# A fused Mamba-2 block on one core: the decay products taken from bf16 parts, and the second decay and attention moved one block later

## The chip, the core and the metric

The kernel runs on one NeuronCore of a Trainium2 chip. The metric is the device time in microseconds, the median of several runs. Shorter is better. The engines are TensorE (PE in the profile, its weight loads PEld), VectorE (DVE), ScalarE (ACT), GpSimd (POOL) and SyncE (SP, which issues all the DMAs here).

## The reference, cut to what matters

The input is 8 sequences of 256 tokens with 512 channels. Each goes through a layernorm, an RMS norm, a Mamba-2 mixer, a gated MLP of width 1792, a second layernorm, a linear layer with a routed LoRA and a last layernorm. The change touches the mixer's decay only:

```python
a = (dt * A).reshape(B, c, Q, H).transpose(0, 1, 3, 2)      # Q = 128 tokens a chunk, H = 4 heads
cs = jnp.cumsum(a, axis=-1)
tri = jnp.tril(jnp.ones((Q, Q), bool))
Ldec = jnp.where(tri, jnp.exp(cs[..., :, None] - cs[..., None, :]), 0.0)
att = jnp.einsum('bchqn,bchkn->bchqk', Cc, Bc) * Ldec
Yd = jnp.einsum('bchqk,bchkp->bchqp', att, Xdt)
...
Yo = jnp.einsum('bchqn,bchpn,bchq->bchqp', Cc, prev, jnp.exp(cs))
```

The exponent cs[q] - cs[k] is the sum of a over the tokens after k up to q. The kernel gets it as a matrix product: a mask times `ra`, where `ra` is a spread over the triangle (`ra[k, h, q] = a[k, h]` for k <= q). There are three such products in a sequence: one for each of the two chunks of 128 tokens, with the mask `below`, and one with the mask `ones` for exp(cs) of the second chunk.

## The kernel before

A sequence of 256 tokens is a group g, and there are 8. The work is a software pipeline of steps t = 1 to 9 (`steps`). In step t the mixer (part a) works on group t, the MLP (part b) on group t-1, and the last layers (part c) on group t-2. Group 0's mixer, together with the scaling and splitting of the weights, runs ahead of the steps in the functions `first`, and `head(g)` is true for group 0 alone.

A step has 14 blocks f = 0 to 13, one for each block of 128 MLP channels. Every engine has its own hand-written order of work. In block f each of PE, ACT and DVE first does its share of the MLP for f and then what the tables `A_AT` (mixer), `C_AT` (last layers) and `NEXT_AT` (next group) name for f. On PE the MLP's share is `b_gu(f)` (gate and up, 24 products into a bank of `GU`) and then `b_down(f-1)` (6 products into `ACC`). For block f ACT computes the silu (`b_silu`, L721), DVE multiplies (`b_prod`, L1111), ACT writes the upper half (`b_hi`, L731) and DVE the lower half (`b_lo`, L1116) of `act`, for which `b_down(f)` waits. `b_gu(f)` waits for `b_prod(f-2)`. Engines meet through semaphores, and each engine works strictly in its own order, so whatever stands behind a waiting instruction waits too.

GpSimd has no blocks. Its order in a step is: `norm_c(c, 1)` (L523: two tiny instructions that give the inverse deviation for a norm of part c), `b_copy` (L521), `a_xd` (L493: four products y = D * x), `a_scan_in` (L477: two instructions that write `ra`), `a_tdt` (L485: two instructions that spread dt over the triangle into `hn`), `norm_c(c, 2)`, `a_xw` (L500), `a_ce` (L508), `a_norm`, `a_rms` and `norm_c(c, 3)`.

These are the places around the change:

- DVE, block 2: `a_dt` ends with `a_t` (L1045), for which `a_scan_in` waits. Block 3: `a_h0` (L987) and `c_stats2`. Block 4: `c_h3` (L1140, which waits for `norm_c(c, 2)`) and `c_lo3` (L1162). Block 5: `a_dec` for both chunks (L1055, L1059) and `a_att` of the first (L1064). Block 6: `a_att` of the second and `c_route`.
- ACT, block 4: `a_tok`, both `a_exp` (L689) and then `c_hi3` (L737, after `c_h3`). Block 6: the third `a_exp`. Changes between Exp and Silu cost an ACT_TABLE_LOAD.
- PE, block 4: `a_tok`, `a_dec(0)`, `a_dec(1)`. Block 5: `a_att(0)`, `a_dec(2)`. Block 6: `a_att(1)`, `a_state` and `c_logits`. All matrix products show as L1368, the line of the helper `mm`.

A float32 product appears in the trace as two MATMUL records.

Of the kernel before, what the change touches and what calls it, by code (L numbers as in the profile page):

```python
# [102 lines left out]
def build(nc, x, w_in, w_dt, w_out, w_gate, w_up, w_down, w_lin, w_gl, lora_b, cols, rows, ln_rows, out):  # L103
# [3 lines left out]
    with ctx:  # L107
        def sb(name, shape, dt=F32):
            return ctx.enter_context(nc.sbuf_tensor(name, shape, dt))
# [6 lines left out]
        def sem(name):  # L116
            if name not in made:
# [41 lines left out]
        a_t = sb("a_t", [P, TILES, H])  # L159
        ra = sb("ra", [P, TILES, H, P])  # L160
        dec = sb("dec", [P, TILES, H, P])
# [14 lines left out]
        rows_1, rows_2, rows_3 = [t.bitcast(F16).rearrange("p (t s d) -> p t s d", t=TILES, s=2)  # L176
                                  for t in (ra[:].rearrange("p t h q -> p (t h q)"),
                                            xbc[:, 0:4].rearrange("p c q -> p (c q)"),
# [92 lines left out]
        def head(g):  # L271

            return g == 0
# [166 lines left out]
        def _(pool):  # L440
# [31 lines left out]
            def a_scan_in(g):  # L472
                pool.wait_ge(sem("a_ready"), g + 1)
                for j in range(TILES):
                    if j == 0:
                        prev(g, 3, 3, pool, sem("dec_ps_ready"))
                    nc.gpsimd.tensor_tensor(ra[:, j], tri[:].unsqueeze(1).broadcast_to([P, H, P]),  # L477
                                            a_t[:, j].unsqueeze(2).broadcast_to([P, H, P]), ALU.mult)\
                        .then_inc(sem("ra_ready"), 1)

            def a_tdt(g):
# [53 lines left out]
            def step(a, b, c):  # L535
                if c is not None and alone(c):
                    return
                if c is not None:
                    chain_c.group(c)
                    norm_c(c, 1, 1.0)  # L540
                if b is not None:
                    b_copy(b)
                if a is not None:
                    a_xd(a)
                    a_scan_in(a)
                    a_tdt(a)
                if c is not None:
                    norm_c(c, 2, ACT_SCALE)
                if a is not None:
                    a_xw(a)  # L550
                    a_ce(a)
                    if a + 1 < GROUPS:
                        a_norm(a + 1)
                    a_rms(a)
                if c is not None and not held(c):
                    norm_c(c, 3, 1.0)
                    chain_c.close()
# [28 lines left out]
        def _(eng):  # L586
# [165 lines left out]
            def c_u(g, j):  # L752
# [5 lines left out]
                    3: lambda g: (a_silu(g, 2), a_z(g, 1)),  # L758
                    4: lambda g: (a_tok(g), a_exp(g, 0), a_exp(g, 1)), 6: lambda g: (a_exp(g, 2), a_state(g)),
                    8: lambda g: a_sumsq(g, 0), 9: lambda g: a_sumsq(g, 1), 11: lambda g: a_hi2(g)}  # L760
# [72 lines left out]
        def _(dve):  # L833
            setup = Chain(dve, sem("dve_setup"), 0)
            setup.group(0)

            chain_a = Chain(dve, sem("dve_a"), 17)
            chain_stats = Chain(dve, sem("dve_stats"), 3)
            chain_c = Chain(dve, sem("dve_c"), 19)
# [190 lines left out]
            def a_dt(g):  # L1030
# [4 lines left out]
                for c in (0.0, 1.0 / 3, -0.5, 1.0):  # L1035
                    if c:
                        chain_a(nc.vector.scalar_tensor_tensor(t, t, c, e, ALU.add, ALU.mult))
                    else:
# [7 lines left out]
                                        ALU.mult).then_inc(sem("a_ready"), 1)  # L1046

            def flat(t):
                return t.rearrange("p h q -> p (h q)")
# [187 lines left out]
            def c_out(g):  # L1237
                c_norm(g, 3, h3, h3, sem("n3_ready"))
                for j in range(TILES):
# [3 lines left out]
            A_AT = {0: lambda g: a_conv(g, 0), 1: lambda g: (a_conv(g, 1), a_dtv(g)),  # L1243
                    2: lambda g: (a_conv(g, 2), a_dt(g)), 3: lambda g: a_h0(g),
                    5: lambda g: (a_dec(g, 0), a_dec(g, 1), a_att(g, 0)), 6: lambda g: a_att(g, 1),
                    7: lambda g: (a_y(g, 0), a_y(g, 1)), 8: lambda g: a_h1(g, 0),
# [5 lines left out]
            def step(a, b, c):  # L1252
# [4 lines left out]
                if a is not None:  # L1257
                    chain_a.group(a)
                for f in range(FBLK):
                    if a == 1:  # L1260
                        prepare(f)
                    if b is not None:
                        b_prod(b, f)
                        b_lo(b, f)
                    if a is not None and f in A_AT:
                        A_AT[f](a)
                    if c is not None and f in C_AT:
                        C_AT[f](c)
                    if a is not None and a + 1 < GROUPS and f in NEXT_AT:
                        NEXT_AT[f](a + 1)  # L1270
# [95 lines left out]
        def _(pe):  # L1366
# [95 lines left out]
            def a_dec(g, n):  # L1462
# [7 lines left out]
                else:  # L1470
                    pe.wait_ge(sem("exp_ready"), g * 3 + 1)
                mm(dec_bank(g, n)[:], (below if n < TILES else ones)[:], flat(ra[:, min(n, 1)]), True, True)\
                    .then_inc(sem("dec_ps_ready"), 1)

# [130 lines left out]
            def last():  # L1605
# [11 lines left out]
                for j in range(TILES):  # L1617
                    c_lora(LAST, j)

            A_AT = {0: lambda g: g > 1 and a_in(g, 1), 1: lambda g: (a_in(g, 2), a_dt(g)), 2: lambda g: a_z(g, 0),  # L1620
                    3: lambda g: a_z(g, 1), 4: lambda g: (a_tok(g), a_dec(g, 0), a_dec(g, 1)),
                    5: lambda g: (a_att(g, 0), a_dec(g, 2)), 6: lambda g: (a_att(g, 1), a_state(g)),
                    7: lambda g: (a_y(g, 0), a_y(g, 1)), 8: lambda g: a_o(g, 0), 9: lambda g: a_o(g, 1)}
# [124 lines left out]
```

## Time and profile before

| | us |
|---|---|
| median of 3 runs (795.97 to 797.41) | 795.98 |
| the profiled execution | 792.34 |
| its span, first to last instruction | 790.6 |

| engine | busy us | share of the span |
|---|---|---|
| PE | 755.6 | 96% |
| PEld | 532.0 | 67% |
| DVE | 485.1 | 61% |
| ACT | 332.5 | 42% |
| POOL | 152.7 | 19% |

Busy time is the union of the records of an engine. A timeline merges neighbouring instructions of one kind and gives the start, the time that the merged stretch took, engine, line, operation, output <- input, shapes and count. A bracket at its end tells how long the engine sat idle before it and what released it. Starts and durations are in us from the start of the span. The time of the profiled execution is 1.7 us above its span.

### The profile page before, as it was taken

What the parts mean: (1) busy time and instruction counts of PE and PEld (TensorE: products, weight loads), DVE (VectorE), ACT (ScalarE), POOL (GpSimd) and SP (SyncE); (2) the same over time, 40 slices, a digit from 0 to 9 for tenths busy, and PEclk for the clock granted to TensorE, in tenths of its full rate; (3) what the DMA queues carried; (4) which work ended last, traced back from release to release, by engine and by line L of the source; (5) the groups of instructions that cost most, each with busy time, mean ns of one, the idle gap of its engine ahead of it and who ended that gap; (6) DMA issues with size and microseconds to landing.
All of it is one profiled execution on the core that took longest, in us unless ns stands there. A gap on an engine that the chain in (4) does not pass through costs nothing.

```text
span 790.6 us, 13864 instructions
## 1 busy us (share of the span) xinstructions
PE 755.6 (96%) x5558; PEld 532.0 (67%) x5558; DVE 485.1 (61%) x1109; ACT 332.5 (42%) x607; POOL 152.7 (19%) x199
## 2 busy tenths in 40 slices
PE   3898989999999999999999999999999999999995
PEld 3676756677667866687656876578666876667752
DVE  5988877866545764476645765457644766255356
ACT  2944675536332562335523363325613264222221
POOL 1220411033110340015110330105210231001021
PEclk9999999999999999999999999999999999999996
DMA  8960000301003020210104020220202101031001
GB/s 313 388 223 1 1 27 1 80 2 40 15 14 94 1 55 1 54 55 27 28 1 82 28 54 1 31 77 1 56 0 54 55 2 27 1 80 31 25 0 54
DMA packets 60081, 41.12 MB, mean 52 GB/s; under 512 B 45680, under 2 KB 45808, under 8 KB 60016
## 3 DMA queue, kind: packets, MB, share of 16 engines
q1 hardware_dynamic: 60016, 40.22, 18.3%
q8 instruction: 44, 0.72, 0.4%
q14 instruction: 21, 0.17, 0.1%
HBM read 25.01 MB, written 4.19 MB: 37 GB/s over the span
## 4 chain that ended last, share of the span: by engine, by line
PE 84%; DVE 10%; ACT 2%; issue 1%; DMA 1%; POOL 0%; SPq 0%; ACTq 0%; DVEq 0%
PE gu L1368 34%; PE wa L1368 24%; PE acc L1368 19%; PE wc L1368 6%; DVE weights L938 3%; DVE xbc L1011 2%; DMA weights<-in_w_in 1%; DVE sg L1111 1%; DVE stats_a L1167 0%; ACT act L731 0%; ACT weights L604 0%; PE wc L1583 0%; DVE hn L1173 0%; DVE act L1116 0%; PE wa L1456 0%
## 5 line engine op out<-in xcount | busy, mean ns | idle before, releaser
L1368 PE MATMUL gu<-h2t,weights 128*128 128x256 f16 x2688 | 311.6, 273 | 1.0 <-DVE h2t L1105 1.0
L1368 PEld LDWEIGHTS gu<-h2t,weights 128*128 128x128 f16 x2688 | 260.2, 98 | 55.6 <-issue 19.3
L1368 PE MATMUL acc<-weights,act 128*128 128x512 f16 x672 | 163.4, 379 | 8.8 <-DVE act L1116 8.8
L1111 DVE SCALAR_TENSOR_TENSOR sg<-gu,bound,sg 128x256 f32<-128x256 f32 x112 | 53.6, 478 | 117.6 <-ACT sg L721 116.9
L721 ACT ACTIVATE sg<-gu,scale_inv 128x256 f32<-128x256 f32 x112 | 53.0, 473 | 159.8 <-PE gu L1368 159.6
L1368 PEld LDWEIGHTS acc<-weights,act 128*128 128x128 f16 x672 | 65.2, 98 | 66.2 <-DVE act L1116 10.9
L1368 PE MATMUL wa<-ht,weights 128*128 128x256 f16 x912 | 105.4, 273 | 0.4 <-DVE h L1079 0.4
L1368 PEld LDWEIGHTS wa<-ht,weights 128*128 128x128 f16 x912 | 89.0, 98 | 16.8 <-issue 0.8
L731 ACT ACTIVATE act<-sg 128x256 f16<-128x256 f32 x112 | 46.6, 416 | 90.8 <-DVE sg L1111 90.8
L1116 DVE TENSOR_TENSOR act<-sg,act 128x256 f16<-128x256 f32 x112 | 50.6, 451 | 54.1 <-ACT act L731 54.1
L1011 DVE SCALAR_TENSOR_TENSOR xbc<-wa,conv_ws,xbc 128x253 f32<-128x253 f32 (+1 forms) x132 | 57.3, 475 | 2.0 <-ACT xbc L643 0.5
L1368 PE MATMUL wa<-w_out_t,y 128*128 128x512 f32 x128 | 57.6, 592 | 0.0
L463 POOL TENSOR_SCALAR small_c<-mv_c 128x2 f32<-128x2 f32 x21 | 4.0, 192 | 223.8 <-DVE mv_c L955 223.8
L938 DVE SCALAR_TENSOR_TENSOR weights<-weights,scale_v 128x512 f16<-128x512 f32 x56 | 41.1, 787 | 6.0 <-ACT weights L604 5.8
L1368 PEld LDWEIGHTS wa<-w_out_t,y 128*128 128x128 f32 x128 | 24.2, 190 | 25.0 <-issue 23.0
L493 POOL TENSOR_SCALAR y<-xbc,rows_t 128x256 f32<-128x256 f32 x28 | 32.8, 1186 | 35.1 <-ACT xbc L654 35.1
L643 ACT ACTIVATE xbc<-wa,cols_t,conv_ws 128x256 f32<-128x256 f32 x48 | 24.3, 559 | 34.7 <-PE wa L1368 34.7
L604 ACT ACTIVATE weights<-weights,scale_v 128x512 f16<-128x512 f32 x56 | 36.3, 712 | 1.6 <-DVE weights L938 0.9
L699 ACT ACTIVATE hn<-h 128x512 f32<-128x512 f32 x16 | 10.1, 630 | 59.9 <-DVE h L1079 59.9
L463 POOL TENSOR_SCALAR small_a<-mv_a 128x2 f32<-128x2 f32 (+1 forms) x22 | 5.3, 239 | 149.2 <-DVE mv_a L955 94.8
L1368 PE MATMUL wc<-weights,h3t 128*128 128x512 f16 x144 | 33.0, 379 | 0.0
L1079 DVE TENSOR_TENSOR h<-wa,h 128x512 f32<-128x512 f32 x16 | 11.1, 691 | 35.4 <-PE wa L1368 35.3
(214 smaller groups left out, 822.8 us busy)
## 6 DMA issues: line engine op xcount, KB each, us to landing
xa<-in_x SPq DMA_DIRECT2D x9, 512.0 KB, 3.8
weights<-in_x SPq DMA_DIRECT2D x7, 512.0 KB, 3.7
out_x<-h SPq DMA_DIRECT2D x14, 256.0 KB, 2.4
weights<-in_w_in SPq DMA_DIRECT2D x5, 512.0 KB, 7.9
weights<-in_w_down SPq DMA_DIRECT2D x3, 768.0 KB, 12.8
weights<-in_w_gate SPq DMA_DIRECT2D x2, 1024.0 KB, 12.4
weights<-in_w_up SPq DMA_DIRECT2D x2, 1024.0 KB, 13.9
weights<-in_w_gate SPq DMA_DIRECT2D x2, 768.0 KB, 13.9
```

The source lines that it names most:

```text
L493: nc.gpsimd.tensor_scalar(y[:, h], xbc[:, 0], rowt[:, 4 + h:5 + h], None, ALU.mult)\
L604: nc.scalar.activation(Wh[:, u, 0], W[:, u + SHIFT], ACT.Copy, scale=sv[:, t:t + 1])\
L643: nc.scalar.activation(xbc[:, c], src[:, m * SEQ:(m + 1) * SEQ], ACT.Identity, bias=conv_b[:, c:c + 1], scale=cw[:, c * TAPS + TAPS - 1:c ...
L699: nc.scalar.activation(hn[:, j], h01[:, j], ACT.Square, accum_out=ss[:, 0, j:j + 1])\
L721: nc.scalar.activation(sg[:, f % 2], GU[f % 2][:, 0:SEQ], ACT.Silu, scale=inv_gate)\
L731: nc.scalar.activation(act[:, slot(f), 0], sg[:, f % 2], ACT.Copy)\
L938: nc.vector.scalar_tensor_tensor(Wh[:, u, 1], W[:, u + SHIFT], sv[:, t:t + 1], Wh[:, u, 0], ALU.mult, ALU.subtract).then_inc(split, 1)
L1011: ins = nc.vector.scalar_tensor_tensor(xbc[:, c, late:], conv_in(g, c)[:, 0:SEQ - late], cw[:, c * TAPS + k:c * TAPS + k + 1], xbc[:, c, l ...
L1079: nc.vector.tensor_tensor(h01[:, j], o_bank(g, j)[:], h01[:, j], ALU.add)\
L1111: nc.vector.scalar_tensor_tensor(sg[:, f % 2], GU[f % 2][:, SEQ:2 * SEQ], up_to_act, sg[:, f % 2], ALU.mult, ALU.mult).then_inc(sem("prod_ ...
L1116: nc.vector.tensor_tensor(act[:, slot(f), 1], sg[:, f % 2], act[:, slot(f), 0], ALU.subtract)\
L1368: return nc.tensor.matmul(dst, left, right, start=start, stop=stop)
```

## The change

For groups 1 to 7 `a` is split into three bf16 parts (four small DVE instructions, `a_parts_of`), GpSimd spreads all three over the triangle (`a_spread`, in place of `a_scan_in`), and each decay product becomes three bf16 products with bf16 masks, accumulated in one bank. In GpSimd's order `a_xd` goes behind the spread and `a_tdt`. `a_dec(1)` goes from block 4 to block 5 on PE, its `a_exp` from block 4 to 5 on ACT, and DVE's `a_dec(1)` from block 5 to 6. Group 0 is computed as before.

```diff
-        ra = sb("ra", [P, TILES, H, P])
+        a_parts = sb("a_parts", [P, TILES, 3, H], BF16)
+        a_rest = sb("a_rest", [P, TILES, H])
+        scan = sb("scan_in", [P, TILES, 3, H, P], BF16)
+        ra = scan[:].rearrange("p t n h q -> p (t n h q)")[:, 0:2 * TILES * H * P].bitcast(F32)\
+            .rearrange("p (t h q) -> p t h q", t=TILES, h=H)
...
             def a_scan_in(g):
                 pool.wait_ge(sem("a_ready"), g + 1)
                 for j in range(TILES):
-                    if j == 0:
-                        prev(g, 3, 3, pool, sem("dec_ps_ready"))
                     nc.gpsimd.tensor_tensor(ra[:, j], tri[:].unsqueeze(1).broadcast_to([P, H, P]),
...
+            def a_spread(g):
+                pool.wait_ge(sem("parts_ready"), g)
+                for j in range(TILES):
+                    if j == 0:
+                        pool.wait_ge(sem("dec_ps_ready"), g * 3)
+                    nc.gpsimd.tensor_tensor(
+                        scan[:, j].rearrange("p n h q -> p (n h) q"),
+                        upper(tri[:]).unsqueeze(1).broadcast_to([P, 3 * H, P]),
+                        a_parts[:, j].rearrange("p n h -> p (n h)").unsqueeze(2).broadcast_to([P, 3 * H, P]),
+                        ALU.mult).then_inc(sem("ra_ready"), 1)
...
                 if a is not None:
+                    a_spread(a)
+                    a_tdt(a)
                     a_xd(a)
-                    a_scan_in(a)
-                    a_tdt(a)
                 if c is not None:
                     norm_c(c, 2, ACT_SCALE)
...
-                    4: lambda g: (a_tok(g), a_exp(g, 0), a_exp(g, 1)), 6: lambda g: (a_exp(g, 2), a_state(g)),
+                    4: lambda g: (a_tok(g), a_exp(g, 0)), 5: lambda g: a_exp(g, 1), 6: lambda g: (a_exp(g, 2), a_state(g)),
...
+            def a_parts_of(g):
+
+                dve.wait_ge(sem("a_ready"), g + 1)
+                chain_p(nc.vector.tensor_copy(a_parts[:, :, 0], a_t[:]))
+                chain_p(nc.vector.tensor_tensor(a_rest[:], a_t[:], a_parts[:, :, 0], ALU.subtract))
+                chain_p(nc.vector.tensor_copy(a_parts[:, :, 1], a_rest[:]))
+                nc.vector.tensor_tensor(a_parts[:, :, 2], a_rest[:], a_parts[:, :, 1], ALU.subtract)\
+                    .then_inc(sem("parts_ready"), 1)
...
-                    2: lambda g: (a_conv(g, 2), a_dt(g)), 3: lambda g: a_h0(g),
-                    5: lambda g: (a_dec(g, 0), a_dec(g, 1), a_att(g, 0)), 6: lambda g: a_att(g, 1),
+                    2: lambda g: (a_conv(g, 2), a_dt(g), a_parts_of(g)),
+                    3: lambda g: a_h0(g),
+                    5: lambda g: (a_dec(g, 0), a_att(g, 0)), 6: lambda g: (a_dec(g, 1), a_att(g, 1)),
...
-                mm(dec_bank(g, n)[:], (below if n < TILES else ones)[:], flat(ra[:, min(n, 1)]), True, True)\
-                    .then_inc(sem("dec_ps_ready"), 1)
+                left, j = below if n < TILES else ones, min(n, 1)
+                if head(g):
+                    last = mm(dec_bank(g, n)[:], left[:], flat(ra[:, j]), True, True)
+                else:
+                    for part in range(3):
+                        last = mm(dec_bank(g, n)[:], upper(left[:]), flat(scan[:, j, part]), part == 0, part == 2)
+                last.then_inc(sem("dec_ps_ready"), 1)
...
-                    3: lambda g: a_z(g, 1), 4: lambda g: (a_tok(g), a_dec(g, 0), a_dec(g, 1)),
-                    5: lambda g: (a_att(g, 0), a_dec(g, 2)), 6: lambda g: (a_att(g, 1), a_state(g)),
+                    3: lambda g: a_z(g, 1), 4: lambda g: (a_tok(g), a_dec(g, 0)),
+                    5: lambda g: (a_dec(g, 1), a_att(g, 0), a_dec(g, 2)), 6: lambda g: (a_att(g, 1), a_state(g)),
```

## Rows read from the trace of the kernel before

**Rows 1.** The page: busy time of each engine and its share of the span.

```profile
PE 755.6 (96%) x5558; PEld 532.0 (67%) x5558; DVE 485.1 (61%) x1109; ACT 332.5 (42%) x607; POOL 152.7 (19%) x199
```

**Rows 2.** Windows: stretch, length, busy of PE, PEld, DVE, ACT, POOL, granted clock, DMA.

```profile
87.00:168.00 81.00, 74.42 (x510) 52.39 (x509) 60.47 (x116) 47.83 (x85) 14.61 (x14) 1.00 0.11 27
260.00:351.00 91.00, 91.00 (x664) 64.17 (x662) 53.23 (x123) 37.24 (x68) 18.88 (x23) 1.00 0.15 36
```

**Rows 3.** Timeline of PE, blocks 4 to 6 of step 3 (group 3).

```profile
279.44 1.46 PE L1368 MATMUL acc<-weights,act 128*128 128x512 f16 x6
...
281.06 1.88 PE L1368 MATMUL wa<-ra,below 128*128 128x512 f32 x4
282.78 2.78 PE L1368 MATMUL gu<-h2t,weights 128*128 128x256 f16 x24
285.40 1.46 PE L1368 MATMUL acc<-weights,act 128*128 128x512 f16 x6
286.69 1.02 PE L1368 MATMUL wa<-xbc 128*128 128x512 f32 x2
...
291.03 1.46 PE L1368 MATMUL acc<-weights,act 128*128 128x512 f16 x6
```

**Rows 4.** Timeline of DVE in the same stretch, blocks 2 to 5.

```profile
276.15 0.17 DVE L1045 TENSOR_TENSOR a_t<-dts,neg_a 128x8 f32<-128x8 f32 x1
...
277.20 0.53 DVE L1116 TENSOR_TENSOR act<-sg,act 128x256 f16<-128x256 f32 x1 [0.48 <-ACT act L731]
277.65 2.44 DVE L987 TENSOR_SCALAR h<-xa,mv_a,small_a 128x512 f32<-128x512 f32 x2
...
282.75 1.00 DVE L1140 TENSOR_SCALAR h<-weights,mv_c,small_c 128x512 f32<-128x512 f32 x2
...
288.98 0.42 DVE L1116 TENSOR_TENSOR act<-sg,act 128x256 f16<-128x256 f32 x1 [0.48 <-ACT act L731]
```

**Rows 5.** Timeline of POOL in step 3; the second row is one of four.

```profile
265.06 4.72 POOL L493 TENSOR_SCALAR y<-xbc,rows_t 128x256 f32<-128x256 f32 x4 [2.73 <-ACT xbc L654]
...
267.06 0.92 POOL L493 TENSOR_SCALAR y<-xbc,rows_t 128x256 f32<-128x256 f32 x1
...
276.40 2.22 POOL L477 TENSOR_TENSOR ra<-tri,a_t 128x512 f32<-128x512 f32 x2 [6.62 <-DVE a_t L1045]
278.58 2.40 POOL L485 TENSOR_TENSOR hn<-tri,dts 128x512 f32<-128x512 f32 x2
281.65 0.19 POOL L463 TENSOR_SCALAR small_c<-mv_c 128x2 f32<-128x2 f32 x1 [0.67 <-DVE mv_c L955]
```

**Rows 6.** Timeline of ACT in the same stretch, behind both decays.

```profile
285.04 1.15 ACT L737 ACTIVATE weights<-h 128x512 f16<-128x512 f32 x2
286.21 1.28 ACT L721 ACT_TABLE_LOAD   x1
287.50 0.47 ACT L721 ACTIVATE sg<-gu,scale_inv 128x256 f32<-128x256 f32 x1
```

**Rows 7.** Timeline of step 1, blocks 3 and 4, DVE and PE.

```profile
95.22 3.64 DVE L938 SCALAR_TENSOR_TENSOR weights<-weights,scale_v 128x512 f16<-128x512 f32 x3
...
100.96 0.99 DVE L987 TENSOR_SCALAR h<-xa,mv_a,small_a 128x512 f32<-128x512 f32 x2
101.09 1.47 PE L1368 MATMUL acc<-weights,act 128*128 128x512 f16 x6 [3.75 <-DVE act L1116]
101.87 2.06 DVE L938 SCALAR_TENSOR_TENSOR weights<-weights,scale_v 128x512 f16<-128x512 f32 x3
```

**Rows 8.** Windows of 4 us near the end, columns as in Rows 2.

```profile
768.00:772.00 4.00, 2.23 (x12) 1.15 (x11) 3.19 (x7) 1.28 (x2) 2.12 (x4) 0.97 0.00 0
772.00:776.00 4.00, 2.86 (x31) 1.51 (x30) 3.16 (x13) 0.60 (x1) 0.89 (x2) 0.50 0.01 4
776.00:780.00 4.00, 4.00 (x14) 1.49 (x12) 3.76 (x13) 0.00 (x0) 0.00 (x0) 0.68 0.00 0
```

**Rows 9.** Groups by form: a one-input copy on POOL, busy us and mean ns.

```profile
L521 POOL COPY h1b<-h 128x1024 f32<-128x1024 f32 x8 | 9.2, 1155 | 0.0
```

More of the change, by code:

```diff
@@ L176, in build @@
         rows_1, rows_2, rows_3 = [t.bitcast(F16).rearrange("p (t s d) -> p t s d", t=TILES, s=2)
-                                  for t in (ra[:].rearrange("p t h q -> p (t h q)"),
+                                  for t in (ra.rearrange("p t h q -> p (t h q)"),
                                             xbc[:, 0:4].rearrange("p c q -> p (c q)"),
@@ L837, in _ @@
             chain_a = Chain(dve, sem("dve_a"), 17)
+            chain_p = Chain(dve, sem("dve_parts"), 3)
             chain_stats = Chain(dve, sem("dve_stats"), 3)
@@ L1258, in step @@
                     chain_a.group(a)
+                    chain_p.group(a - 1)
                 for f in range(FBLK):
```

## The prediction, made before the changed kernel was run

> **What bounds the kernel now.** I read the busy times first: PE is busy for 96% of the span and no other engine for more than 67% [rows 1]. The windows by step then say where the other 4% lie. Step 3 (260 to 351 us) has PE busy for all of its 91.0 us at a granted clock of 1.00, and steps 2 to 7 repeat it. Step 1 (87 to 168 us) has only 74.4 of 81, because DVE and ACT still split weights there [rows 2]. So from step 2 on every microsecond taken from PE is a microsecond of time, if nothing that PE waits for comes later than now; and each order has to be followed instruction by instruction, since a cover of a few microseconds is all that hides the other engines. I took step 3 as the pattern. Its PE timeline shows gu(5), down(4), what block 5 has of the mixer, gu(6) and down(5), and no row of it has a bracket for idle time [rows 3].
>
> **What PE saves.** A float32 product of 512 columns is two records. Four of them start at 281.06 and the next work at 282.78, so one product takes 0.86 us. Six 16-bit records of 512 columns start at 285.40 and the next work at 286.69, or 0.215 each [rows 3]. Three bf16 products are then 0.645 us. Three decays a group save 3 x 0.215 = 0.64 us, over 7 groups 4.5 us. That is all that the change can gain. No row shows a bf16 product with these masks; the 16-bit products beside it are the nearest, and their weight loads are hidden.
>
> **What DVE adds.** Four instructions on 8 to 24 elements, one waiting for the other. `a_t` of that size takes 0.17 us [rows 4]; with the waits I take 0.2 each, 0.8 us (bounds 0.7 and 1.2). They stand ahead of block 3's multiply. The lower half that comes of it is ready at 277.73 [rows 4] and PE's down(3) takes it at 279.44 [rows 3], so 1.7 us of PE's own work hide the 0.8 us in steps 2 to 7; without that cover they cost 0.8 us each time. GpSimd starts its spread at 277.2 in place of 276.40 [rows 5].
>
> **What GpSimd adds.** Each spread has 1536 elements a partition in place of 512. Two of the old ones take 2.22 us, and two `a_tdt` of the same form 2.40 [rows 5]. That is 1.11 to 1.20 us for 512. bf16 elements on GpSimd are in no row; I take the float32 price by element, 3.4 us for one spread and 6.8 us for both. The lower bound is that of a one-input copy, 1.16 us for 1024 [rows 9], so 1.7 and 3.5 us. The upper bound is the slowest row by element, `a_xd` with 0.90 us for 256 [rows 5], so 5.4 and 10.8 us. I stay with 6.8 since operation and broadcasts are the same as in the old row. The first decay product finds its parts at 280.6 and PE comes at 281.06, so no wait there; the second, one block later, comes at 285.6 and has them since 284.0. That is what the later block covers.
>
> The Trainium skill ("GPSIMD Engine Reference", § Elementwise — side-by-side cycle accounting) says that a two-input operation takes about 2.6 cycles an element at 1.2 GHz, bound by the shared read port and so by elements, not bytes. By that page alone one spread would be an estimated 3.3 us, and bf16 would bring no relief; the old float32 rows agree with its rate.
>
> **What is moved.** This decides the case. Up to now GpSimd did `a_xd` (4.72 us, from 265.06) while it had to wait for `a_t` anyway. Now these four instructions stand behind the spread and `a_tdt`, and ahead of `norm_c(c, 2)`, which started at 281.65 and was right behind its input [rows 5]. DVE's `c_h3` waits for it in block 4, and started at 282.75 [rows 4]. From now on:
>
> - spreads 277.2 to 284.0; `a_tdt` 2.4, to 286.4;
> - `a_xd` at 0.92 each, since DVE is idle by then, 3.7, to 290.1 (4.7 if it is slowed as now);
> - `norm_c(c, 2)` to the start of `c_h3`: 282.75 - 281.65 = 1.1, so `c_h3` starts at 291.2, 8.4 us later than now.
>
> Behind `c_h3` on DVE stand `c_lo3`, block 5's multiply and `a_dec`; behind `c_hi3` on ACT stands block 5's silu. So: the first half of `c_h3` 0.5, ACT's two `c_hi3` 1.15, the table load 1.28 and, from the start of the silu to the end of DVE's lower half, 289.40 - 287.50 = 1.9 [rows 4, 6]. With 0.05 for semaphores that gives 296.1 as the time from which down(5) can start. PE would be there at 291.03 - 0.64 = 290.4 [rows 3]. It waits 5.7 us, and is 5.1 us behind the old time. Nothing on PE can fill that: gu(6) is already done, and down(5) is next in its order.
>
> **Behind that wait.** ACT has to load the Exp table, do the second exponential and load Silu again, where one load takes 1.28 us [rows 6]. By that `a_att(1)`, and then `a_state` behind `a_xw`, come about when PE does; I add 0.1 us for them (bounds 0 and 1). Of the later half of the step (`c_route`, both `a_y`, and the transposes of `rows_3` with those of the next group behind them on SP) I take each as still covered, since PE has 3 to 4 us of MLP work in each block between them. So the step is 5.2 us longer on full clock. It happens in each step with both an a and a c part, steps 2 to 7: 6 x 5.2 = 31.2 us.
>
> **The clock.** The profile shows one fall in the middle of work: around 768 to 772, with PE busy for 2.23 of 4 us, the granted clock leaves 1.00 and is 0.50 (1.2 GHz) in the next window, although PE is busy for 2.86 of 4 us there, and it comes back in the window after [rows 8]. It stayed at 1.00 through the single gap of 3.75 us in step 1 [rows 2, 7]. A gap of 5.7 us is longer than any in the steps before, so I expect a fall in most of them. The fall lasted some 6.8 us; part of that lies inside the gap. At half speed each microsecond of work costs half a microsecond more. Bounds are 0 (no fall) and 3.4 us (none of it inside the gap); with half of it inside I take 1.7 us, 6 x 1.7 = 10.2 us.
>
> The Trainium skill says the same of the mechanism ("TensorE: Matmul & The Clock Gate", § Part 1: The HAM clock gate): an idle TensorE is throttled to 1.2 GHz, and activity releases it. By it every gap of this length would be followed by slow products; by the step 1 row alone a gap may pass without.
>
> **Step 1** has no part c, so no such wait. But DVE is late there: down(3) waits 3.75 us for it [rows 7], so the four new instructions cost their 0.8 at once. While GpSimd works DVE is slow: three lower halves take 3.64 us beside it and 2.06 without, and `a_h0` takes 2.44 for two beside it and 0.99 without [rows 4, 7]. GpSimd now works some 9 us longer behind `a_t` (4.6 for the spreads, the rest `a_xd`), so both costs (some 1.5 each) come on top; I take more than half of them as covered by the work that PE has before down(4). With two more table loads on ACT (2.6 us, of which perhaps 1 us shows) and 0.64 saved I take +2.4 us, with bounds of -0.6 and +6.
>
> **Sum.** 31.2 + 10.2 + 2.4 = 43.8 us. On the profiled execution's 792.3 us this gives 836.1. That execution is 3.6 us under the median of the runs, and the same sum on 795.98 gives 839.8. I predict 840.
>
> **The rivals.**
>
> - Wait without a fall of the clock: 31.2 + 2.4 = 33.6, so 829.6 us. For it: the gap in step 1 that left the clock alone. Against it: that gap was 2 us shorter. Chance 0.15.
> - bf16 is cheap on GpSimd: both spreads take 3.5 us. The chain is 3.3 us earlier, PE waits 2.4 us, the clock holds, and a step is 1.9 us longer: 11.4 + 2 = 13, so 809 us. For it: the copy moves twice the elements in the same time. Against it: it has one input. Chance 0.08.
> - bf16 is dear on GpSimd, at the rate of `a_xd`: both spreads take 10.8 us. Each step loses 4 us more, and the first decay's wait of 1.6 us is swallowed by the larger one: 43.8 + 24 = 68, so 864 us. Chance 0.10.
> - The other side: the cover holds and the gain stays. For that the spreads would have to take 6.8 - 5.7 = 1.1 us together, the point from which PE no longer waits at down(5). Then 4.5 us are saved, so 791.5 us, or somewhat more with step 1. No row on GpSimd is near 3072 elements in 1.1 us. Chance 0.02; and 0.02 for a result within the noise.
>
> The forecast itself, wait and fallen clock, has 0.63. Its bounds are 6 x (4.6 + 0) + 0 = 28 and 6 x (6.0 + 3.0) + 5 = 59, so 824 to 855. For 8 in 10 I take 820 to 860: it holds the forecast and the first rival, together 0.78, and part of the dear one. 0.2% is about what a measurement of this kernel tells from no change. Slower by more 0.96, within 0.02, faster 0.02.
>
> **What would show it.** In the changed trace: PE idle before down(5), that is before an `acc` product, some 5 to 6 us in each of steps 2 to 7, released by DVE `act`; POOL idle no more between `a_tdt` and `norm_c(c, 2)`, with `a_xd` between them and `small_c` at the end; DVE idle some 8 us before L1140's successor, waiting for POOL `small_c`; spreads of 3.4 us; a granted clock under 1.00 in each step. I am wrong if the spreads take much less or more than 3.4 us, if the waits are there and the clock stays at 1.00, or if PE's busy time in a step falls by 0.6 us and nothing else changes.

## The result, and the profile after

| | before | after |
|---|---|---|
| median, 4 runs each (us) | 796.69 (795.97 to 797.90) | 828.09 (826.32 to 829.81) |
| the profiled execution | 792.34 | 829.81 |
| its span | 790.6 | 828.1 |

The ratio of after to before is 1.0392, with a 95% interval of 1.0362 to 1.0423. The change makes the kernel 31.4 us slower, inside the stated range, but 12 us less than the 840 forecast.

Busy time by engine, from the page of the changed kernel (against [rows 1]):

```profile
PE 760.4 (92%) x5564; PEld 531.7 (64%) x5579; DVE 515.6 (62%) x1137; ACT 351.9 (42%) x621; POOL 166.2 (20%) x199
```

PE has 92% of the span in place of 96%. The 4.8 us more of busy time are not more work. They lie in the start of the kernel, ahead of step 1 (54.55 against 49.68 us), where the granted clock was 0.93 in place of 1.00. In a step PE is busy as long as before, 91.25 against 91.22 us, though it has less to do: where PE stops, the tail of the product ahead of the gap counts as busy (0.16 us, since a gu lasts 2.78 us and the next product starts after 2.62 [rows 3]). The loss is idle time. To see where it comes in I took the starts of `b_copy` (the only COPY on POOL, once a step) as marks of the steps:

| start of `b_copy` in step | 1 | 2 | 3 | 4 | 5 | 6 | 7 | 8 |
|---|---|---|---|---|---|---|---|---|
| before | 64.79 | 169.96 | 261.15 | 352.37 | 443.57 | 534.77 | 625.99 | 712.85 |
| after | 70.96 | 182.64 | 278.11 | 373.60 | 469.07 | 564.54 | 660.00 | 751.13 |

A step was 91.2 us and is 95.48, so about 4.27 us longer; the six steps 2 to 7 (the last by the same amount) make 25.6 us. Step 1 went from 105.17 to 111.68, 6.5 us. Behind the last mark the changed kernel takes 0.8 us less. That is 31.3 us, the difference of the medians to 0.1. The 0.8 are hardly the change's: in the other profiles the stretch behind the last mark takes 76.8 to 78.3 us, in these two 77.75 and 76.97. Nor is the first mark. It lies between 64 and 71 us in all profiles here, and goes with the granted clock ahead of it: at 1.00 it is at 64.4 and 64.8 (e6 and before), at 0.90 to 0.97 it is at 67 to 71 in all others. That fits a profiled execution of before that lies 4 us under its median.

One whole step of the changed kernel, as in [rows 2]:

```profile
278.11:373.60 95.49, 91.25 (x666) 63.68 (x667) 57.66 (x128) 40.11 (x70) 20.69 (x25) 1.00 0.14 34
```

The clock is 1.00: in steps 2 to 7 it never fell. The timeline of the same step, PE first (block 3's down, block 4's, block 5's), beside which [rows 3] has the same work of before:

```profile
297.26 1.47 PE L1393 MATMUL acc<-weights,act 128*128 128x512 f16 x6 [0.70 <-DVE act L1139]
...
304.08 1.47 PE L1393 MATMUL acc<-weights,act 128*128 128x512 f16 x6 [1.76 <-DVE act L1139]
305.39 0.81 PE L1393 MATMUL wa<-scan_in,below 128*128 128x512 bf16 x3
...
311.90 1.47 PE L1393 MATMUL acc<-weights,act 128*128 128x512 f16 x6 [1.57 <-DVE act L1139]
```

PE now waits three times for the lower half of `act`: 0.70, 1.76 and 1.57 us, together 4.0, or 4.5 with the tails of 0.16. Less the 0.65 that PE saves, down(5) is 3.9 us late, and some 0.4 more comes behind it in small steps of 0.1. The third row is a decay product: three bf16 records, 305.39 to 306.04, so 0.65 us. PE's own saving is there as forecast. DVE and GpSimd in that stretch (against [rows 4] and [rows 5]):

```profile
294.97 2.23 DVE L1139 TENSOR_TENSOR act<-sg,act 128x256 f16<-128x256 f32 x1 [0.48 <-ACT act L744]
297.12 4.15 DVE L1001 TENSOR_SCALAR h<-xa,mv_a,small_a 128x512 f32<-128x512 f32 x2
...
306.90 1.00 DVE L1163 TENSOR_SCALAR h<-weights,mv_c,small_c 128x512 f32<-128x512 f32 x2 [2.87 <-POOL small_c L468]
```

```profile
294.17 5.64 POOL L488 TENSOR_TENSOR scan_in<-tri,a_parts 128x1536 bf16<-128x1536 bf16 x2 [14.89 <-DVE a_parts L1068]
299.77 2.40 POOL L498 TENSOR_TENSOR hn<-tri,dts 128x512 f32<-128x512 f32 x2
302.16 3.62 POOL L506 TENSOR_SCALAR y<-xbc,rows_t 128x256 f32<-128x256 f32 x4
305.87 0.19 POOL L467 TENSOR_SCALAR small_c<-mv_c 128x2 f32<-128x2 f32 x1
```

Two things are to be seen. `c_h3` starts at 306.90, released by GpSimd's `small_c`, and `small_c` started 0.1 us behind `a_xd`. That is the chain of the prediction. But further up DVE's lower half of block 3 takes 2.23 us, where [rows 4] has 0.53, and the two `a_h0` take 4.15 us where they took 2.44, both beside the two spreads. The prediction had no such thing. The first two waits of PE come from there, as e5 shows below. The spreads themselves take 5.64 us, not 6.8.

Step 1, blocks 2 and 3 (against [rows 7]):

```profile
102.07 7.05 DVE L952 SCALAR_TENSOR_TENSOR weights<-weights,scale_v 128x512 f16<-128x512 f32 x3
102.23 6.34 POOL L488 TENSOR_TENSOR scan_in<-tri,a_parts 128x1536 bf16<-128x1536 bf16 x2 [30.24 <-DVE a_parts L1068]
...
111.36 2.74 PE L1393 MATMUL acc<-weights,act 128*128 128x512 f16 x6 [7.83 <-DVE act L1139]
```

Three lower halves of weights take 7.05 us in place of 3.64, and PE waits 7.83 us in place of 3.75.

### The profile page after: what moved, and what is told of

Same layout as the page of the kernel before. It is cut to its first block, busy times and chain, and to the rows that moved or that the text cites. A ratio compares the mean times of both kernels' runs of the same rounds, so it can differ in the third digit from the quotient of the medians.

```text
span 828.1 us, 13940 instructions
## 1 busy us (share of the span) xinstructions
PE 760.4 (92%) x5564; PEld 531.7 (64%) x5579; DVE 515.6 (62%) x1137; ACT 351.9 (42%) x621; POOL 166.2 (20%) x199
## 4 chain that ended last, share of the span: by engine, by line
PE 53%; issue 14%; DVE 14%; POOL 10%; ACT 5%; DMA 2%; SPq 1%; POOLq 0%; ACTq 0%; DVEq 0%
PE gu L1393 21%; PE wa L1393 14%; PE acc L1393 13%; PE wc L1393 5%; POOL scan_in L488 4%; DVE xbc L1025 3%; DVE weights L952 3%; POOL y L506 3%; POOL hn L498 2%; DMA weights<-in_w_up 2%; DVE sg L1134 1%; ACT L734 1%; ACT act L744 1%; DVE stats_c L967 1%; ACT sg L734 1%
## 5 line engine op out<-in xcount | busy, mean ns | idle before, releaser
L1393 PE MATMUL wa<-ht,weights 128*128 128x256 f16 x912 | 107.2, 275 | 0.4 <-DVE h L1102 0.4
L1139 DVE TENSOR_TENSOR act<-sg,act 128x256 f16<-128x256 f32 x112 | 59.3, 530 | 54.0 <-ACT act L744 54.0
L488 POOL TENSOR_TENSOR scan_in<-tri,a_parts 128x1536 bf16<-128x1536 bf16 x14 | 40.2, 2890 | 119.5 <-DVE a_parts L1068 119.5
L952 DVE SCALAR_TENSOR_TENSOR weights<-weights,scale_v 128x512 f16<-128x512 f32 x56 | 45.0, 857 | 6.5 <-ACT weights L617 6.3
```

Source lines behind the costliest of these rows:

```text
L488: nc.gpsimd.tensor_tensor(scan[:, j].rearrange("p n h q -> p (n h) q"), upper(tri[:]).unsqueeze(1).broadcast_to([P, 3 * H, P]), a_parts[:, ...
L952: nc.vector.scalar_tensor_tensor(Wh[:, u, 1], W[:, u + SHIFT], sv[:, t:t + 1], Wh[:, u, 0], ALU.mult, ALU.subtract).then_inc(split, 1)
L1139: nc.vector.tensor_tensor(act[:, slot(f), 1], sg[:, f % 2], act[:, slot(f), 0], ALU.subtract)\
L1393: return nc.tensor.matmul(dst, left, right, start=start, stop=stop)
```

## The experiments

Two theories were to be told apart. The order theory says that the loss is `c_h3` waiting for `norm_c(c, 2)` behind `a_xd`. The hold theory says that the long spreads keep DVE's instructions with two SBUF inputs, or with one input where the instruction uses both port pairs (as `c_h3`, 1.00 us alone and 2.44 beside GpSimd in e9), from running. In this table a step is the distance of two marks in steps 3 to 6 (for e4 the mean), and step 1 that of the first two. The ratio is to the kernel before on the same chip.

| run | edit | median | before | ratio (95%) | step | step 1 |
|---|---|---|---|---|---|---|
| before | | | 796.69 | | 91.2 | 105.2 |
| after | | 828.09 | 796.69 | 1.0392 (1.0362 to 1.0423) | 95.5 | 111.7 |
| e1 | after, `a_xd` first | 817.17 | 797.17 | 1.0258 (1.0238 to 1.0277) | 93.75 | 110.9 |
| e2 | before, `a_xd` late | 798.04 | 797.17 | 1.0015 (0.9998 to 1.0031) | 91.3 | 105.95 |
| e3 | before, later block | 798.06 | 797.17 | 1.0013 (0.9998 to 1.0027) | 91.2 | 106.7 |
| e4 | after, `a_xd` twice | 860.21 (1 run) | 797.17 | | 100.86 | 111.7 |
| e5 | e1, spreads in three | 810.22 | 796.09 | 1.0177 (1.0155 to 1.0199) | 92.6 | 110.5 |
| e6 | e1, both spreads in one | 830.25 | 796.09 | 1.0415 (1.0381 to 1.0449) | 95.75 | 111.4 |
| e7 | after, group 1 as before | 824.33 | 796.09 | 1.0362 (1.0334 to 1.0390) | 95.5 | 107.5 |
| e8 | e5 and e7's edit | 806.21 | 796.09 | 1.0129 (1.0107 to 1.0152) | 92.6 | 106.7 |
| e9 | e8, `norm_c` before `a_tdt` | 802.48 | 797.22 | 1.0067 (1.0048 to 1.0086) | 91.9 | 107.2 |
| e10 | e9, `a_tdt` after `c_lo3` | 793.71 | 797.22 | 0.9946 (0.9924 to 0.9967) | 90.57 | 106.7 |

### e1: the order undone

```diff
                 if a is not None:
+                    a_xd(a)
                     a_spread(a)
                     a_tdt(a)
-                    a_xd(a)
```

> The changed kernel with a_xd back at its old place, ahead of the spread. Two theories of the 4.3 us that each of steps 2 to 7 is longer (91.2 before, 95.5 after). Order theory: the loss is c_h3 waiting behind a_xd; then only GpSimd's longer spread is left in that chain, a step is about 91 us, and the median is about 802 (what step 1 lost stays). Hold theory: the two 2.8 us spreads hold back DVE's lower half of block 3 and a_h0, so PE's waits before down(3) and down(4), 0.7 and 1.8 us, stay and only the one before down(5), 1.6 us, and what follows it go; a step is about 93.2 us and the median about 815.

```profile
292.14 2.23 DVE L1139 TENSOR_TENSOR act<-sg,act 128x256 f16<-128x256 f32 x1 [0.48 <-ACT act L744]
294.43 1.47 PE L1393 MATMUL acc<-weights,act 128*128 128x512 f16 x6 [0.70 <-DVE act L1139]
...
301.26 1.47 PE L1393 MATMUL acc<-weights,act 128*128 128x512 f16 x6 [1.76 <-DVE act L1139]
...
307.34 1.47 PE L1393 MATMUL acc<-weights,act 128*128 128x512 f16 x6
```

The first two waits are unchanged to the hundredth, the third is gone, and DVE's lower half is held for 2.23 us as before. The median is 817.17, near the 815 of the hold theory and 15 us above the 802 of the order theory. So the order is 1.7 us of the 4.27 a step.

### e2 and e3: two parts of the change alone

```diff
                 if a is not None:
-                    a_xd(a)
                     a_scan_in(a)
                     a_tdt(a)
+                    a_xd(a)
```

> The kernel before with nothing but a_xd moved behind a_tdt. If the move costs what it adds ahead of norm_c, each step is 3 us longer and the median about 815. By the chain of the prediction c_h3 starts at 285.8 in place of 282.75, the lower half of block 5 is ready at 290.7 and PE comes at 291.03: hidden, a step stays 91.2 to 91.5 us and the median is 796 to 799. Then the move costs only together with the longer spread.

The wait of `c_h3` is there, and still PE waits for nothing:

```profile
288.24 3.64 POOL L493 TENSOR_SCALAR y<-xbc,rows_t 128x256 f32<-128x256 f32 x4
289.69 0.43 DVE L1116 TENSOR_TENSOR act<-sg,act 128x256 f16<-128x256 f32 x1 [0.48 <-ACT act L731]
...
293.00 1.00 DVE L1140 TENSOR_SCALAR h<-weights,mv_c,small_c 128x512 f32<-128x512 f32 x2 [2.88 <-POOL small_c L464]
...
297.51 0.43 DVE L1116 TENSOR_TENSOR act<-sg,act 128x256 f16<-128x256 f32 x1 [0.48 <-ACT act L731]
...
298.31 1.46 PE L1368 MATMUL acc<-weights,act 128*128 128x512 f16 x6
```

The lower half of block 5 is ready at 297.94, and PE comes to down(5) at 298.31. The cover of 0.4 us is just enough; the median is 0.9 us up, and the interval reaches to no change. With longer spreads in front, it is not enough. The second row bears on the hold: DVE's lower half lies beside `a_xd`, whose instructions have one large input, and takes the 0.43 us that it takes alone.

e3 moves the second decay, its exponential and DVE's `a_dec` to the later block in the kernel before, in the three tables of the diff, and nothing else.

> The kernel before with nothing but the second decay, its exponential and DVE's second a_dec one block later. Two more table loads on ACT in each group. If they are hidden, steps 2 to 7 stay at 91.2 us and step 1 grows by up to 1 us: median 796 to 798. If ACT's 2.6 us show, a step is up to 2.6 us longer and the median up to 812.

It costs nothing in steps 2 to 7 and 1.55 us in step 1, where I had expected up to 1. ACT's two more table loads are hidden in steps 2 to 7. The interval of the ratio reaches to no change here too.

### e4: a longer single gap, for the clock

```diff
             def a_xd(g):
                 pool.wait_ge(sem("o_ps_ready"), g * 2)
                 pool.wait_ge(sem("xbc_ready"), g * 3 + 1)
+                for h in range(H):
+                    nc.gpsimd.tensor_scalar(y[:, h], xbc[:, 0], rowt[:, 4 + h:5 + h], None, ALU.mult)\
+                        .then_inc(sem("xd_first"), 1)
+                pool.wait_ge(sem("xd_first"), g * 4)
                 for h in range(H):
```

> The changed kernel with a_xd done twice over (same values), 3.6 us more ahead of norm_c(c, 2) in each step. This lengthens the one wait of PE before down(5) from 1.6 to about 5.2 us. If a single gap of that size makes the granted clock fall, as the prediction had it, windows of the steps show less than 1.00 and a step is 3.6 us plus up to 1.7 longer: about 860. If it doesn't fall, 3.6 us longer: about 849.

The gap at down(5) of step 3, and the windows around it (columns as in [rows 2]):

```profile
318.22 2.74 PE L1397 MATMUL acc<-weights,act 128*128 128x512 f16 x6 [5.28 <-DVE act L1143]
```

```profile
314.00:317.00 3.00, 0.00 (x0) 0.00 (x0) 1.74 (x4) 2.71 (x4) 0.00 (x0) 1.00 0.19 39
317.00:320.00 3.00, 1.78 (x5) 0.68 (x6) 2.14 (x5) 2.66 (x4) 0.95 (x1) 0.50 0.71 136
320.00:323.00 3.00, 3.00 (x6) 1.40 (x5) 1.08 (x3) 1.81 (x3) 0.09 (x1) 0.50 0.00 0
323.00:326.00 3.00, 3.00 (x39) 1.99 (x38) 2.20 (x7) 2.46 (x4) 0.52 (x1) 0.86 0.03 5
```

The gap is 5.28 us, and behind it the granted clock is 0.50 (1.2 GHz) and then rises again. In the profile the clock falls in each of steps 2 to 7. A step is 5.4 us longer than that of the changed kernel. By 3.7 the wait before down(5) is longer (5.28 against 1.57), and 1.7 on average, 1.0 to 2.4 by step, is the slow stretch. That is the 1.7 us that the prediction had put in. So its price for the clock was right for a single gap of this size, but the changed kernel has three short gaps with work between them, at which the clock stayed at 1.00 throughout. The Trainium skill ("TensorE: Matmul & The Clock Gate", § Part 1: The HAM clock gate) says that an idle TensorE is throttled; the trace agrees for the gap of 5.28 us, and shows none of it for gaps of 0.7 to 1.8 us.

### e5 and e6: the same elements in shorter and in longer instructions

e5, on top of e1 (PE waits for all three):

```diff
-                    nc.gpsimd.tensor_tensor(
-                        scan[:, j].rearrange("p n h q -> p (n h) q"), ...
+                    for part in range(3):
+                        ins = nc.gpsimd.tensor_tensor(
+                            scan[:, j, part], upper(tri[:]).unsqueeze(1).broadcast_to([P, H, P]),
+                            a_parts[:, j, part].unsqueeze(2).broadcast_to([P, H, P]), ALU.mult)
+                        ins.then_inc(sem("ra_part" if part < 2 else "ra_ready"), 1)
```

> a_xd at its old place and each spread as three instructions of 512 elements in place of one of 1536: the same elements in instructions a third as long. Hold theory (a DVE instruction that reads or writes through both ports cannot run until GpSimd's current instruction ends): the lower half of block 3 takes about 1.2 us in place of 2.2 and each a_h0 about 1 in place of 2.1, PE's waits before down(3) and down(4) go, a step is 90.7 to 91.3 us in place of 93.75, and the median is 797 to 803. Rate theory (DVE is slowed in proportion to GpSimd's busy time, however it is cut): a step stays 93.7 us or is longer by the four more instructions, and the median is 817 or more.

e6, on top of e1:

```diff
-                for j in range(TILES):
...
+                nc.gpsimd.tensor_tensor(
+                    scan[:].rearrange("p t n h q -> p (t n h) q"),
+                    upper(tri[:]).unsqueeze(1).broadcast_to([P, 6 * H, P]),
+                    a_parts[:].rearrange("p t n h -> p (t n h)").unsqueeze(2).broadcast_to([P, 6 * H, P]),
+                    ALU.mult).then_inc(sem("ra_ready"), 2)
```

> a_xd at its old place and both spreads as one instruction of 3072 elements, twice as long. Hold theory: the lower half of block 3 is held for the whole 5.6 us, so it takes about 5 us and PE waits about 3.5 us before down(3); a_h0 then runs beside a_tdt only and is shorter, so a step is 1 to 2 us longer than 93.75, and the median is 823 to 830. Rate theory: a step stays at 93.7 us and the median at 817.

The timeline of e6, GpSimd's one spread, DVE's lower half of block 3 and PE's down(3) with the first and the second decay product, and two windows behind it (columns as in [rows 2]):

```profile
287.60 5.31 POOL L486 TENSOR_TENSOR scan_in<-tri,a_parts 128x3072 bf16<-128x3072 bf16 x1 [7.49 <-issue]
288.34 4.85 DVE L1137 TENSOR_TENSOR act<-sg,act 128x256 f16<-128x256 f32 x1 [0.48 <-ACT act L742]
293.25 2.34 PE L1391 MATMUL acc<-weights,act 128*128 128x512 f16 x6 [3.32 <-DVE act L1137]
...
296.03 1.35 PE L1391 MATMUL wa<-scan_in,below 128*128 128x512 bf16 x3
...
301.13 0.81 PE L1391 MATMUL wa<-scan_in,below 128*128 128x512 bf16 x3
```

```profile
294.00:297.00 3.00, 3.00 (x10) 1.50 (x9) 2.97 (x7) 0.00 (x0) 1.27 (x2) 0.50 0.08 12
298.00:301.00 3.00, 3.00 (x25) 2.22 (x23) 1.54 (x4) 2.97 (x5) 0.12 (x1) 1.00 0.24 91
```

The spread ends at 292.91 and the DVE instruction, begun at 288.34, ends at 293.19, 0.28 us behind it. The same DVE instruction takes 0.53 us beside pieces of 512 elements (e5), 2.23 beside 1536 (e1) and 4.85 beside 3072 (e6). GpSimd's work is the same each time. So DVE is not slowed in proportion to what GpSimd does; it is held until the running GpSimd instruction ends. The other two traces show the same end: the DVE instruction is done 0.3 us behind the start of GpSimd's next one (286.97 and 286.64 us in e8, whose pieces are those of e5, 297.20 and 296.88 in the changed kernel). The Trainium skill has this rule ("SBUF — State Buffer", § Who interferes with whom): the second port pair of VectorE is shared with GpSimd as an exclusive lock, held for a whole instruction, and a VectorE instruction with two SBUF inputs or in a 2-port mode has to wait for it. The trace agrees, with 0.53, 2.23 and 4.85 us, for GpSimd's two-input products; beside `a_xd` in e2 the same instruction was not held. I had not weighed it.

The wait of e6 before down(3) is as forecast (3.32 us), and so is the step, 2.0 us longer than e1's, but that second agreement is luck. I had left out the clock, and behind the gap of 3.32 us it is at 0.50 for some 4 us in each of steps 2 to 7: the decay product takes 1.35 us in place of 0.81, and from down(3) to down(4) PE needs 6.58 us where e10 needs 4.88. The 1.7 us between them are the clock's, so the longer hold itself added only 0.3 us to the step. The median of 830.25 lies just above the 830 expected.

In e5 the waits before down(3) and down(4) are gone too, but its step is 92.6 and not the 91.3 that I expected: the median of 810 lies between the two theories' figures. A wait of 1.53 us before down(5) has come back, since six instructions take longer than two. The same step in e8, where it is the only wait of PE left, shows what it hangs on:

```profile
285.65 6.58 POOL L491 TENSOR_TENSOR scan_in<-tri,a_parts 128x512 bf16<-128x512 bf16 x6 [7.44 <-DVE a_parts L1070]
286.44 0.53 DVE L1141 TENSOR_TENSOR act<-sg,act 128x256 f16<-128x256 f32 x1 [0.48 <-ACT act L746]
...
295.52 1.00 DVE L1165 TENSOR_SCALAR h<-weights,mv_c,small_c 128x512 f32<-128x512 f32 x2 [3.02 <-POOL small_c L468]
...
300.52 1.47 PE L1395 MATMUL acc<-weights,act 128*128 128x512 f16 x6 [1.54 <-DVE act L1141]
```

The spreads take 6.58 us in place of 5.64. Behind them come `a_tdt` (2.2) and then `norm_c(c, 2)`, so `c_h3` waits 3.02 us for it. The hold went, and the order theory's wait took its place, now behind `a_tdt`.

### e7 and e8: step 1

e7 gives group 1 what group 0 has, in the changed kernel:

```diff
-                    a_spread(a)
+                    a_spread(a) if a > 1 else a_scan_in(a)
...
-                    2: lambda g: (a_conv(g, 2), a_dt(g), a_parts_of(g)),
+                    2: lambda g: (a_conv(g, 2), a_dt(g), g > 1 and a_parts_of(g)),
...
-                if head(g):
+                if g < 2:
```

> The changed kernel with group 1 computed as group 0: float32 spread and products, no parts (a_xd and the later block stay). Step 1 took 111.7 us from b_copy to b_copy, against 105.2 before. Hold theory: it is the two long spreads beside DVE's splitting of the weights; without them step 1 is back to 105 to 107 us and the median is 828 - 5.5 = 822 to 824, with the 7.8 us wait before down(3) back to about 3.7. If the move of a_xd or the table loads cost step 1, it stays above 109 and the median above 826.

Step 1 is 107.5 us in place of 111.7: of the 6.5 us the parts and their spreads are 4.2. The other 2.3 are as much as e2 and e3 show alone, 0.8 and 1.55, though e7's profile has a fall of the clock in step 1 that those two haven't, so the sum may fit by chance. Step 1 and the median of 824.33 are just above what I expected (107 and 824).

Cutting the spreads does not do the same for step 1. In e5 the first three lower halves of weights are back at 3.64 us, but GpSimd's six pieces and `a_tdt` now last until 112.3 us, and beside them the two `a_h0` take 2.44 us and the next three halves 3.63, where they took 0.99 and 2.06 [rows 7]. Step 1 is 110.5 us against 110.9 in e1. One DVE instruction beside short pieces is hardly held; a row of them is held at each piece.

e8 takes e1, e5 and e7 together.

> The three together: a_xd first, spreads cut in three, group 1 in float32. If hold and order are all that the change costs, what PE saves is left: 6 steps by 0.64 us less what the later block costs (0.9 us in its own run), so 792.5 to 796 against 796.7. If bf16 parts cost PE or DVE elsewhere, 797 to 800.

Missed: 806.21. I had taken the two causes to be all, and had not asked what is late next once they go. It was the wait shown above.

### e9 and e10: the rest of the order, and the last collision

```diff
                     a_spread(a) if a > 1 else a_scan_in(a)
-                    a_tdt(a)
                 if c is not None:
                     norm_c(c, 2, ACT_SCALE)
                 if a is not None:
+                    a_tdt(a)
```

> The kernel with all three edits, and norm_c(c, 2) also ahead of a_tdt. With the three edits a step was 92.6 us: the waits before down(3) and down(4) were gone and one of 1.5 us before down(5) was left, with c_h3 waiting 3.0 us for norm_c behind a_tdt (2.2 us). If that order is what is left, c_h3 starts 2.2 us earlier, the last wait goes and a step is 90.7 to 91.1 us: median 795 to 797.5 against 796.1. If the two more table loads and DVE's later a_dec hold PE elsewhere, a step stays above 91.5 and the median above 799.

Missed again, in part: a step is 91.87, the median 802.48.

```profile
290.13 2.22 POOL L500 TENSOR_TENSOR hn<-tri,dts 128x512 f32<-128x512 f32 x2
290.20 2.44 DVE L1165 TENSOR_SCALAR h<-weights,mv_c,small_c 128x512 f32<-128x512 f32 x2 [0.89 <-POOL small_c L468]
...
296.57 1.47 PE L1395 MATMUL acc<-weights,act 128*128 128x512 f16 x6 [0.78 <-DVE act L1141]
```

`c_h3` starts as early as expected, but now beside `a_tdt`, and takes 2.44 us where it took 1.00. Half of what the order gave was taken back by the hold, and 0.78 us of PE's wait is left. e10 adds one wait, so that GpSimd starts `a_tdt` only when DVE has finished `c_lo3`:

```diff
                     norm_c(c, 2, ACT_SCALE)
+                    pool.wait_ge(sem("h3_split"), c * 2 + 2)
                 if a is not None:
                     a_tdt(a)
```

> The kernel of the last run with one wait more: GpSimd starts a_tdt only when DVE has done c_h3 and c_lo3 (h3_split), so that no GpSimd work lies beside them. In the last run c_h3 took 2.44 us beside a_tdt in place of 1.00, and PE still waited 0.78 us before down(5). Hold theory: c_h3 is back to 1.0 us, that wait goes, a_tdt still ends about when a_dec wants it, and a step is 91.0 to 91.2 in place of 91.87: median 798 to 799 against 797, so the change still gains nothing. If a_tdt comes too late for a_dec, PE waits before a_state or a_att(1) instead and a step stays at 91.8 or more.

```profile
291.90 1.00 DVE L1166 TENSOR_SCALAR h<-weights,mv_c,small_c 128x512 f32<-128x512 f32 x2 [0.89 <-POOL small_c L468]
...
294.51 2.04 POOL L500 TENSOR_TENSOR hn<-tri,dts 128x512 f32<-128x512 f32 x2 [2.65 <-DVE weights L1188]
...
297.33 1.46 PE L1396 MATMUL acc<-weights,act 128*128 128x512 f16 x6
```

`c_h3` takes 1.00 us, `a_tdt` is done at 296.55, 0.2 us before `a_dec` takes it at 296.76, and down(5) has no bracket: PE waits for nothing in the step. A step is 90.57 us, which is 91.2 less the 0.64 us of the bf16 products. I had expected 91.0 and no gain. The median is 793.71 against 797.22, a ratio of 0.9946 (0.9924 to 0.9967), so this version beats both kernels. By the marks, six steps save 0.64 us each, 3.8 us, and step 1 loses 1.5; the rest of the 3.5 us lies ahead of the first mark and behind the last. In the kernel before PE waits for nothing in these steps, so the new order alone could not have saved them: what is saved is the bf16 products.

## Why the prediction was right, and where it was not

The direction and the range held, but the forecast itself, one long wait and a fallen clock, did not. The +43.8 us came out as +31.4, so that the measured 828.1 us lies nearest to the first rival (a wait without a fall, 829.6 us, chance 0.15). Two of its own signs failed: the wait before down(5) is 1.57 us and not 5 to 6, and the clock stays at 1.00 with waits there. By its own steps:

- **What PE saves:** 0.64 us a group. Right: three bf16 records take 0.65 us, and e10's step is shorter by just that.
- **What DVE adds:** 0.8 us for four instructions. Right in size, and hidden, as e10 shows, where PE waits for nothing with them in place. But the cover of 1.7 us ahead of down(3) did not hold: the lower half behind them took 2.23 us in place of 0.53, so PE waited 0.70 before down(3). The step that failed here is that I gave GpSimd's longer work a price on GpSimd and on the chain behind it and none on DVE in steps 2 to 7, though I had used that very effect for step 1. e1, e5 and e6 show it.
- **What GpSimd adds:** 6.8 us for both spreads, measured 5.64. The term was 1.16 us too high, over six steps 7.0 us. 512 elements of bf16 take 1.10 us each (e8), like float32 with 1.11 [rows 5], but 1536 take 2.8 and 3072 take 5.31 (e6): bf16 is about as dear, and by these three part of each instruction's time does not grow with its length. The other estimate given there, 3.3 us for one spread, was too high as well.
- **What is moved:** the chain from `a_xd` over `norm_c`, `c_h3`, ACT and the silu to down(5) came out to a tenth. From `c_h3` to down(5) it had 4.9 us and took 5.0, and with the measured spread it gives down(5) 3.9 us late against the mark; it was 3.9 late. But what was one gap of 5.7 us in the forecast were three waits, 0.70, 1.76 and 1.57. The first two only use up time that PE would have waited at the third. That is why e1, which removes the cause that I named, gives back 10.9 of 31.4 us: behind the chain the hold was already waiting, 2.5 us a step.
- **Behind that wait:** 0.1 us, and the step lost 4.27 where the chain alone gives 3.94. That is 0.33 us in small waits, before `a_att(1)`, before `a_state` and within `a_y`, 0.23 us a step too low, over six steps 1.4 us.
- **The clock:** 10.2 us forecast, none in steps 2 to 7. The price was right for one gap (1.7 us a step at 5.28 us in e4 and at 3.32 us in e6), the condition was not met, because the gap came in three pieces. It did fall in step 1, within the gap of 7.83 us.
- **Step 1:** +2.4 forecast, +6.5 measured. The bound was 6, so this term lies outside its own. Here too it is the hold: three weight halves beside two long spreads took 7.05 us in place of 3.64, and e7 gives back 4.2. The prediction had the effect at 1.5 us for each of two costs, more than half of it covered; the three halves alone took 3.4 us more.

The sum of these, with the 0.8 behind the last mark, is 43.8 - 7.0 - 10.2 + 1.4 + 4.1 - 0.8 = 31.3 us. Two errors of one sign and two of the other: that the number came within 12 us is in part luck. The forecast of a slowdown rested on the chain, which was right, and e2 shows that it decides only together with the longer spread, as the rival on the other side had it (a point up to which the cover holds).

## What to carry to other kernels

Work given to an idle engine is not free if it shares a port: a two-input GpSimd product held back the VectorE instructions that need the shared pair until it ended. So put such work beside VectorE instructions that don't need the pair: in e10 the statistics of `c_stats2` (one input) took 1.27 us and `b_prod` (one input from PSUM) 0.45 beside the spreads, no more than without (1.27 in e6, 0.48). Or cut it into short pieces, which helped in steps 2 to 7 and not in step 1, or fence it off with a wait, as e10 did. When the order on a side engine is changed, ask which small instruction that another engine waits for now stands behind the large ones (here `norm_c`, 1 us of work for which the whole MLP waited). And when one cause is taken away, look for the one right behind it before pricing the gain: here the median went from 828.1 us over 817.2 (e1), 810.2 (e5), 806.2 (e8) and 802.5 (e9) to 793.7 (e10), and only the last edit let the change gain.

## What the runs showed of the hardware

- How long DVE is held goes with the length of the one GpSimd instruction, not with GpSimd's load: 0.53, 2.23 and 4.85 us for the same DVE instruction beside 512, 1536 and 3072 elements. It does not hold for each GpSimd instruction: beside the one-input `a_xd` it took 0.43 us (e2), and 0.66 in another place (block 0 of the kernel before). What decides that, no run shows.
- bf16 brought GpSimd's two-input product no speed at 512 elements (1.10 us, float32 1.11). By element it is 2.15 ns at 512 and 1.73 ns at 3072 (5.31 us); float32 at that length was not run.
- Three gaps of 0.70, 1.76 and 1.57 us in one step left the granted clock at 1.00; one of 5.28 us (e4) and one of 3.32 us (e6) brought it to 0.50 (1.2 GHz) in each of steps 2 to 7.
- For single gaps of that smaller size the length alone does not tell. The gap before down(3) of step 1 is 3.75 us in the kernel before, in e8 and in e9: in the first two the clock stays at 1.00, in e9 it is at 0.50 behind it, and the six products take 2.74 us in place of 1.47.
